# A two-layer attention and expert kernel: layer 1's first score products moved into the tile loop, and the second half's queries made dense

## What is computed

```python
x = x + _L0_xattn_ref(_layernorm(x), ctx_768, ...)   # 16 heads of 8 columns, 128 keys
x = x + _L0_ffn_ref(_layernorm(x), ...)              # 8 experts of width 512, top 1, relu squared
x = x + _L1_xattn_ref(_layernorm(x), ctx_768, ...)   # 16 heads of 8, scores clipped, NaN guard
x = x + _L1_ffn_ref(_layernorm(x), ...)              # 8 experts of width 256, top 2, gelu
```

```python
q = (query @ Wq + bq).reshape(B, Nq, H, D).transpose(0, 2, 1, 3)
k = (key_value @ Wk + bk).reshape(B, Nkv, H, D).transpose(0, 2, 1, 3)
attn = jnp.clip(jnp.einsum('bhqd,bhkd->bhqk', q, k) * scale, -CLAMP, CLAMP)
attn = jax.nn.softmax(attn, axis=-1)
attn = jnp.where(jnp.any(jnp.isnan(attn)), 1.0 / Nkv, attn)
x = jnp.einsum('bhqk,bhkd->bqhd', attn, v).reshape(B, Nq, Cq) @ Wo + bo
```

## Time and profile before

| | |
|---|---|
| median of 3 runs | 232.23 us (232.05 to 233.31) |
| the profiled execution, its own time | 231.29 us |
| its span in the profile | 229.5 us |
| busy: PE / weight loads / DVE / ACT / POOL | 212.9 / 168.8 / 161.1 / 120.1 / 75.7 us |
| mean granted clock of PE | 0.993 |
| end of the tile loop on PE (last `down`) | 116.82 us from the span's start |
| steps 0 to 8 of layer 1's attention on PE | 118.36 to 139.13 us |
| step 10 of it begins | 143.14 us |

### The profile page before, as it was taken

The page is one execution under the profiler, slowest core; times in us unless marked ns, Lnnn a source line. Parts: engine busy times, 40 slices in busy tenths (PEclk is TensorE's granted clock), DMA queues, the critical chain, the costliest instruction groups (busy, mean ns, idle before and its releaser), DMA issues.

```text
span 229.5 us, 6728 instructions
## 1 busy us (share of the span) xinstructions
PE 212.9 (93%) x2522; PEld 168.8 (74%) x2522; DVE 161.1 (70%) x516; ACT 120.1 (52%) x225; POOL 75.7 (33%) x100
## 2 busy tenths in 40 slices
PE   8999987998779999999979899999699999999994
PEld 8666866766458999999875657877568686776774
DVE  1785765877556865577538755798758965799995
ACT  6765554665725655656510386567563275343340
POOL 8820810010530577646351394666600100000000
PEclk9999999999999999999999799999999999999999
DMA  6932118582244016120211110212200000001001
GB/s 216 365 110 51 50 41 276 169 282 85 58 114 95 24 60 175 50 80 26 67 51 48 50 49 28 74 50 71 76 1 0 3 0 0 3 1 46 1 3 46
DMA packets 14116, 17.18 MB, mean 75 GB/s; under 512 B 1684, under 2 KB 10004, under 8 KB 14084
## 3 DMA queue, kind: packets, MB, share of 16 engines
q1 hardware_dynamic: 11732, 13.59, 19.8%
q0 software_dynamic: 1152, 2.24, 3.2%
q10 hardware_dynamic: 1200, 0.92, 1.3%
HBM read 11.18 MB, written 3.95 MB: 66 GB/s over the span
## 4 chain that ended last, share of the span: by engine, by line
PE 71%; DVE 13%; DMA 5%; ACT 3%; issue 3%; POOL 2%; DVEq 0%; POOLq 0%; SPq 0%; ACTq 0%
PE ps L1219 12%; PE ps L1443 12%; PE ps L1455 12%; PE ps L1529 6%; PE ps L1539 5%; PE ps L1278 4%; PE ps L1227 2%; PE ps L1489 2%; DVE mx L785 2%; DVE xn L749 2%; PE ps L1316 2%; PE ps L1292 2%; PE ps L1247 2%; DMA q<-work 2%; PE ps L1180 2%
## 5 line engine op out<-in xcount | busy, mean ns | idle before, releaser
L785 DVE TENSOR_REDUCE mx<-ps 128x4 f32<-128x512 f32 x64 | 41.1, 685 | 19.7 <-PE ps L1219 19.3
L577 ACT ACTIVATE PT<-ps 128x512 f32<-128x512 f32 x64 | 35.6, 590 | 25.9 <-PE ps L1227 25.9
L1219 PE MATMUL ps<-k,q 32*128 32x128 f32 x512 | 37.0, 288 | 4.1 <-DMA q<-mT 1.2
L1219 PEld LDWEIGHTS ps<-k,q 32*128 32x128 f32 x512 | 31.4, 191 | 12.6 <-DVE mx L785 9.7
L1455 PEld LDWEIGHTS ps<-proj,work 128*128 128x128 f32 x256 | 30.7, 192 | 5.7 <-issue 5.7
L713 ACT ACTIVATE work<-ps,fc 128x512 f32<-128x512 f32 x32 | 21.4, 687 | 24.0 <-PE ps L1443 22.5
L1227 PE MATMUL ps<-q,k 32*128 32x128 f32 x512 | 33.6, 288 | 0.3 <-DVE mx L785 0.3
L1455 PE MATMUL ps<-proj,work 128*128 128x128 f32 x256 | 31.1, 275 | 0.0
L445 POOL DMA_INDIRECT moe_y<-ys,tok_i x22 | 22.3, 1012 | 24.0 <-DVE ys L1018 12.0
L1443 PE MATMUL ps<-xT,fc 128*128 128x512 f32 x64 | 30.1, 593 | 0.0
L1227 PEld LDWEIGHTS ps<-q,k 32*128 32x128 f32 x512 | 28.2, 191 | 1.0 <-issue 0.7
(11 more groups left out here) (169 smaller groups left out, 292.5 us busy)
## 6 DMA issues: line engine op xcount, KB each, us to landing
fc<-in_fc SPq DMA_DIRECT2D x8, 256.0 KB, 3.6
proj<-in_proj SPq DMA_DIRECT2D x8, 256.0 KB, 4.2
slots_x<-xs SPq DMA_DIRECT2D x2, 709.5 KB, 7.5
fc<-in_w SPq DMA_DIRECT2D x8, 129.0 KB, 2.2
proj<-in_w SPq DMA_DIRECT2D x8, 128.0 KB, 2.5
k<-work SPq DMA_DIRECT2D x12, 64.0 KB
wr<-in_wr SPq DMA_DIRECT2D x1, 719.5 KB, 7.6
xs<-slots_x SPq DMA_DIRECT2D x2, 322.5 KB, 4.0
```

The costliest lines, as they stand in the source:

```text
L577: nc.scalar.activation(PT[:, j % PTR, :], ps[:, ST_BANK(layer, j), :], ACT.Exp, scale=SCALE).then_inc(b_done, 1)
L785: nc.vector.tensor_reduce(mx[:, b, 4 * g:4 * g + 4], ps[:, S_BANK(layer, j), :].rearrange("p (k m) -> p k m", m=M), axis=AX, op=ALU.max).t ...
L1219: ins = mm(ps[:, S_BANK(layer, 2 * n + i), P * k:P * k + P], q4[r:r + 32, k, L * b:L * b + L], k4[r:r + 32, k, M * b:M * b + M], start=Tru ...
```

## The change

Line numbers in the diff's kernel are some lines higher than before from the middle on; names are the same.

**PE.** The scores of steps 0 and 1 leave the attention loop: step 0's run between `down(20)` and `down(21)`, step 1's right behind `down(21)`. The wait for the last copy out of bank 1 moves to step 3. The scores of steps 8 and 9 leave their place beside the transposed scores of block 2: they run alone, one after the other, in step 9 behind `values(4)`. `second_queries` is one product with packed weights instead of four. The idle product of step 6 is gone.

**DVE.** The maxima of bank 0 are taken between the last square and `y_evac(21)`. Half 1's sum moves from POOL to DVE (`moe_add(1)`), with its statistics behind it, at the head of step 5; the normalisation stands at the head of step 6 (which is the same place in DVE's order). In step 8 the division stands ahead of the maxima, in step 9 the NaN count does.

**ACT and SP.** One copy to `q_dense` in place of four; then ACT issues two of the four spreading transfers and SP the other two (`last_queries_in`, semaphore `q_in_l1b`), SP ahead of the shift row of block 3. SP issues the expert weights from there on one block later. A transfer of zeros (32 KB) stands on SP between the second keys and the slots of half 1.

**Banks and weights.** Steps 0 to 2 write banks 0, 2, 5, 6, 3, 4 instead of 0 to 5. The spread weights of layer 1 (516 of 1439 columns of `wr`) are no longer loaded.

```diff
-        S_BANK = lambda layer, j: j if layer == 1 and j < 6 else j % 3
+        FIRST_S_BANK, EARLY = (0, 2, 5, 6, 3, 4), 2
+        S_BANK = lambda layer, j: FIRST_S_BANK[j] if layer == 1 and j < 6 else j % 3
...
+        def last_queries_in(queue, lo, hi):
+            queue.wait_ge(b_done, ring_no(1, "q"))
+            for g in range(lo, hi):
+                queue.dma_start(q4[32 * g:32 * g + DH, :, N // 2:N], q_dense[32 * g:32 * g + 32, 1, :]).then_inc(q_in[2], 16)
...
@@ SP @@
-                    if layer == 1 and b >= 1:
-                        expert_weights(b - 1)
+                    if layer == 1 and b == 2:
+                        last_queries_in(sp, 0, 2)
+                    elif layer == 1 and b >= 1:
+                        expert_weights(b - 1 if b < 2 else b - 2)
...
             second_keys_in(1)
+            sp.dma_start(q4[DH:P:32, :, N // 2:N], zero_rows[:]).then_inc(q_zeroed, 16)
             slots_in(1)
...
@@ POOL @@
-            pool.wait_ge(gathered[1], 16)
-            pool.wait_ge(top_clip, 2)
-            nc.gpsimd.tensor_tensor(xr[:, HB:B, :], xr[:, HB:B, :], yg[:, HB:B, :], ALU.add).then_inc(b_sum, 1)
...
@@ ACT @@
+            def last_queries_evac():
+                act.wait_ge(q_ps, Q_DONE[1] + 1)
+                nc.scalar.activation(q_dense[:, 1, :], ps[:, ring_at(1, "q"), :], ACT.Identity, bias=wcol(1, "bqd"),
+                                     accum_out=qk_sums[:, 3:4]).then_inc(b_done, 1)
...
                     if layer == 1 and n == 8:
-                        for i in range(4, 8):
-                            queries_evac_ring(i)
+                        last_queries_evac()
+                        last_queries_in(act, 2, 4)
                         o_evac(0)
...
@@ DVE @@
                 for n in range(LAST):
-                    tops(2 * n)
+                    if layer == 1 and n == 5:
+                        moe_add(1)
+                        ln_stats(2, 1)
+                    if layer == 1 and n == 6:
+                        ln_normalise(2, 1)
+                    if layer == 1 and n == 8:
+                        norm(8, 0)
+                    if layer == 1 and n == 9:
+                        guard_count()
+                    if (layer, n) != (1, 0):
+                        tops(2 * n)
...
                 if t == 16:
                     ln_normalise(2, 0)
+            maxima(1, 0)
             y_evac(TILES - 1)
...
@@ PE @@
             def second_queries():
                 pe.wait_ge(ln_xT, XT_NO(2, 1))
-                for i in range(4, 8):
-                    pe.wait_ge(b_done, ring_no(1, ("q", i)) - 3)
-                    mm(ps[:, ring_at(1, ("q", i)), :], wcol(1, "wq")[:, P * (i - 4):P * (i - 4) + P], xT[:, 512:1024],
-                       start=True, stop=True).then_inc(q_ps, 1)
+                pe.wait_ge(b_done, ring_no(1, "q") - 3)
+                mm(ps[:, ring_at(1, "q"), :], wcol(1, "wqd"), xT[:, 512:1024], start=True, stop=True).then_inc(q_ps, 1)
...
+                if layer == 1 and n == 8:
+                    pe.wait_ge(q_in[2], 64)
                 if layer == 1 and n == 3:
-                    pe.wait_ge(s_top, SB(layer, 1))
+                    pe.wait_ge(s_top, SB(layer, 0))
+                    pe.wait_ge(yt_sb, TILES)
...
+                    held = n >= 2 * B or layer == 1 and (n < EARLY or n in (8, 9))
+                    if not held:
+                        scores(layer, n)
...
-                    if layer == 1 and n == 6:
-                        idle_product(512)
                     second_half(layer, n)
...
+                    if layer == 1 and n == 9:
+                        scores_alone(1, 8)
+                        scores_alone(1, 9)
...
+            scores_alone(1, 0)
             down(TILES - 1)
-            pe.wait_ge(yt_sb, TILES)
+            scores_alone(1, 1)
```

114 lines of the change are left out of this document (52 added, 62 removed).

## The result

The changed kernel takes **240.66 us** (median of 4, 239.8 to 243.23) against 232.14 (231.07 to 233.31) for the kernel before on the same chip: ratio 1.038, 95% interval 1.029 to 1.048. Slower, as forecast, but by 8.5 us and not by 2.4; the time lies outside the range of 231.0 to 236.9. The profiled execution took 240.54 us, span 238.8 against 229.5.

What follows compares the result with a forecast made beforehand. PE was taken as the bound (busy 212.9 of 229.5 us). Step 10 starting at 145.6 instead of 143.14 gave +2.4 us, so 231.29 became 233.7; with 0.94 for the median, 234.6 us, range 231.0 to 236.9.

Steps and rivals of the forecast that it cites:

- likeliest case: The forecast itself: waits at the seam and for the last queries both bind, +1.2 to +3.5 us, chance 0.54.
- signs of being wrong: Listed trace signs: `down(21)` within 0.3 us of 116.82, step 8's scores released by m = 5's transposed scores, full clock near 130 us.
- part 4: Dense queries, steps 7 to 10: 2.7 us of PE saved, but waiting for transfers puts step 10 at 145.6, not 143.14: +2.4 us.
- Part 1: Seam between the layers: early scores delay `down(21)` and all behind it 1.2 us, the first transposed scores 0.95 us.
- Part 2: Half 1's sum and norm on DVE: statistics 0.57 us sooner behind the gather, hidden by the exponential's chain, so 0.
- Part 3: Idle product of step 6 removed: gain between 0 and 1.02 us, taken as -0.75 us.
- as if from one queue: Last queries' landing before step 8, if all four transfers run like one queue's: 136.7 + 2.2 + 3.7 = 142.6 us.
- beside each other: Last queries' landing before step 8, if SP's and ACT's queues run in parallel: 136.7 + 0.7 + 3.7 = 141.1 us.
- my middle: The landing time taken for the last queries before step 8: 141.8 us, between 141.1 and 142.6.
- a second fall: Rival: clock falls behind the wait for the last queries, steps 8 to 10 lose up to 1.7 us more: 236.3 us, chance 0.12.
- Quick landings: Rival: spreading transfers at the seam and before step 8 land 2.2 us after issue, +0.35, 232.6 us, chance 0.20.
- The clock stays up: Rival: the half-clock stretch from 128 to 131.5 us gives back up to 1.7 us; faster end 230.9 us, chance 0.14.

Runs made afterwards that it cites:

- e14: The changed kernel, unaltered, run again on another chip: 251.88 us against 243.43 for the kernel before, ratio 1.036.
- e2: The change with half 1's queries by four spread products again, steps 8 and 9 as before, full `wr`: 246.26 us against 244.88 before, ratio 1.025.
- e10: Kernel before with only half 1's sum and norm on DVE, no idle product in step 6, no first-scores wait for the last copy: 244.75 us, ratio 1.023.
- e3: The change with the scores of steps 0 and 1 back behind the last `down`: 248.34 us against 244.88 before, ratio 1.034.
- e7: The change with all four transfers of half 1's queries issued by SP, none by ACT: 248.52 us (one execution) against 245.29 before.
- e6: The change with idle products filling PE's waits in steps 8 and 9: 248.73 us against 245.29 before.
- e8: The change with SP spreading half 0's dense copy two steps early, half 1's own queries not spread: 245.92 us (one execution) against 245.29 before.
- e9: The kernel before, unchanged, traced again on a slower chip: 245.78 us.
- e12: The change with half 0's copy spread earlier by SP, no ACT issues, scores of steps 8 and 9 side by side again: 239.8 us against 244.74, ratio 1.003.
- e5: The changed kernel, unaltered, run again on another chip: 251.1 us against 245.29 for the kernel before.
- e15: The change with ACT's two query transfers on POOL's queue, which adds `bo` two products later: 251.85 us against 246.21 before.
- e1: The change with the unused spread weights of layer 1 loaded again in `wr`: 252.0 us against 244.88 before.

## Why the prediction was right and wrong

**The sign, and where.** Right: slower, by the dense queries, with PE idle ahead of step 8 and the scores of 8 and 9 alone. The likeliest case had it, and the experts keep their length to 0.02 us. But two of the signs of being wrong that I had named came true in the first trace: a row of the clock near 130 us without a fall, and step 8's scores right behind the transposed scores of m = 5. The second is so only because those ran at half clock there (1.91 us); in e14 they took 1.16 and PE then waited 0.85. In the sum, the two first traces differ by 9.3 us where the steps had 2.4: 3.9 us of the surplus lie in part 4. The other 3.0 are 4.6 us in code that was not edited, less 1.7 us ahead of the query product, of which 1.3 are a fall of the clock that did not come.

**Part 1, the seam: +0.95 forecast, +0.3 to +0.5 measured** (e2 against e10, the change against e3). The last transfer of the first spreading landed 4.05 us behind its issue (116.12 to 120.17, in the chain; I took 3.7), so `down(21)` was 1.5 us late and not 1.2. The 2.15 us estimated from the Trainium skill ("DMA: Bandwidth & Descriptors", section "Anatomy of one DMA", whose fit is for transfers that POOL issues) is further off: the trace has nearly twice that. The step that failed is the next one, "+1.2 us for the last copy, the last write of POOL, the gather and all behind it", and it failed twice.

First, the path. I let the attention hang on the gather. The chain of before runs through PE's own products instead, the 1.88 us of idle products in step 3 among them: in the three traces of before the gather went out 8.56, 8.07 and 8.46 us behind the last `up` product, and the first transposed scores came at 11.60 each time. What the seam delays is the scores of step 1, and with them PE's transposition of the first maxima: 8.27 us behind the last `up` product, in e3 7.93. The row behind the gather came in only as a second bound, 0.2 us later, in the first trace.

Second, the size. I took the time from the last write to the gather, 3.94 us in the trace before (118.58 to 122.52), as fixed. It was 3.18 to 3.94 in the seven traces in which the last two writes stood 1.7 us apart, and 2.41 to 2.43 in the eleven in which they stood 3.3 or 3.4 apart. e3 varies the seam alone (3.18). So 1.5 us later writes made a gather 0.8 us later, and none against the one trace I had, which was the longest of the seven. That the later write was held by the earlier is inferred.

**Part 2, the sum:** 0 forecast, with the scores' earlier start -0.41 measured. That start is the dropped wait for the last copy, 0.45 us that I let stop at the gather; it got through to the first transposed scores whole (11.60 to 11.15 us behind `up`). **Part 3, the idle product:** -0.75 forecast, -0.19 measured.

**Part 4, the dense queries.** By its own steps the stretch from the query product to the guard should have grown from 12.59 by 2.25 to 14.85 us. e14 has 19.44, the first trace 18.75. Step by step, with e14's numbers:

- *Landing.* Forecast 7.1 us behind the query product (141.8 less 134.7), measured 7.6: +0.5. The copy was there on time, 1.96 us behind it. From the first issue to step 8's scores it is 5.65 us, near the 5.9 of "as if from one queue" and far from the 4.4 of "beside each other". It is made of ACT's first issue, 1.57 us instead of 0.7, and 4.09 us (151.72 to 155.81), as at the seam. A second issuer saved 0.85 us of landing (e7). The rule of the Trainium skill ("DMA: Bandwidth & Descriptors", section "Issuing engines are not separate DMA queues") agrees better than my middle: I should have taken 142.6.
- *Steps 8 and 9.* Forecast 3.75 us from the landing to step 10, measured 6.27 (155.81 to 162.08): +2.5, with 16 products at 2.08 us in place of 1.16.
- *Steps 10 and 11.* Forecast unchanged, 3.94 us to the guard; measured 5.55: +1.6, all clock.

Together +4.6. With the clock held up the same steps give about 15.6 us (e6), 0.8 over the forecast. So the landing and the waits were sized nearly right, and **the term that failed most is the clock**: the forecast had no fall there, and the rival *a second fall* (chance 0.12) had the mechanism but the wrong price, "up to 1.7 us more", since it took the length of the one fall in the trace, 3.5 us. It lasted 10.2 us in seven of the eight traces with dense queries, waits and no idle products in them (6.8 in e8) and cost 3.0 to 4.0 us where ACT and SP issue as in the change (18.6 to 19.6 less 15.6, an estimate). That it comes from PE's idle time is borne out by e2, e9, e10 and e12 (no wait, no fall in the stretch) and e6 (wait filled, no fall). Why it lasts 10.2 us and not 3.5 no run shows.

**The rest of the 8.5 us.** Measured by the two first traces it is +3.05 in layer 0, +1.53 in the experts, and -1.3 for the fall that the earlier trace rows show and the change's trace lacks. Of these, layer 0 and the experts are code that was not edited. The experts' fall is in that trace and in e6's, and in no other; in e14, e5 and e3 the stretch is 20.83 or 20.84. Layer 0 took 114.0, 124.3 and 128.7 us in three traces of before, and 117.0, 123.9 and 128.3 in three of the change. On two other chips the change cost 5.8 and 6.1 us by the medians. Not settled is why all four executions of the change on the first chip were at a mean clock of 0.951 to 0.964, and with that why it cost 8.5 us there and some 6 elsewhere by the medians, when the ratios are 1.038 and 1.036; 17 us at half clock make 0.964, and the dense queries' fall is 10.2 of them.

**Rivals.** *Quick landings* fell (4.05 us). *The clock stays up* did happen at 128 us, and gave 1.3 us in the first trace, but by luck of the execution: e9, the kernel before, lacks that fall too, and e14 has it. *A second fall* came.

**Two slips** in the sums change nothing: a quarter of 2.48 is 0.62 and not 0.65, and step 7 of the quick landings comes out near 132.9, not 132.75.

**The chances.** A range built from one trace took its clock as the kernel's. The spread of the other sets was not to be seen in three runs within 0.6%; the length of a fall that no row showed was, as an unknown, and its bound should have been far wider than one sample.

## What to carry to other kernels

Saving PE work ahead of a transfer pays only as far as other PE work hides the transfer: here three products were worth 2.6 us, and a chain of copy, issue and landing of some 7.6 us, then two rounds of scores alone with a maximum between them, cost 5.6 at full clock (15.6 less 10.0), then 3 to 4 more in clock. Before a wait is put in the middle of a busy stretch of PE, price the clock behind it as a term of its own, with a length that may be several times that of the falls in the trace. Before a delay is passed down a chain, find in the trace which chain the next wait hangs on: here it was PE's own work and not the gather. And a queue that is given a transfer pays for it in place: ACT's issue held the copy that PE needed next, and POOL's stood behind its clamps.

## What the runs showed of the hardware

- Issuing two 64 KB spreading transfers took ACT 2.26 us (1.53 and 0.69) while SP issued two in 1.82, and SP alone issued four in 3.35 (e7). In the trace before, SP's four took 2.83.
- POOL took 1.27 us to issue two of them (e15).
- The last of the spreading transfers landed 4.05 us behind its issue at the seam, and at most 4.09 us behind it at step 8 (e14).
- POOL's last scattered write reached the gather after 3.18 to 3.94 us when it stood 1.7 us behind another (seven traces), and after 2.41 to 2.43 when it stood 3.3 or 3.4 behind (eleven traces).
- The granted clock stayed at half for 10.2 us behind PE idle times of 1.55 us (first trace, e5), of 1.55 and 0.85 (e14, e3, e1) and of 3.32 (e7), and for 3.5 us near step 4 of before in two of its three traces, not in the third (e9).
